# A post-norm transformer layer in fp32 on one core: the products with V in two groups a unit instead of three

## The reference

```python
q, k, v = (einsum('BSE,EHK->BSHK', x, w) for w in (w_q, w_k, w_v))        # 16 heads of 64
logits = einsum('BSHK,BMHK->BSHM', q, k) / sqrt(64)                        # causal mask
o = einsum('BSHM,BMHK->BSHK', softmax(logits + mask, axis=3), v)
x = layernorm(x + einsum('BSHK,EHK->BSE', o, w_o))
h = gelu(butterfly(x @ W_exp + b_exp, up_weights) + up_bias)               # 512 wide, 9 stages
x = layernorm(x + butterfly(h, down_weights) @ W_con + b_con + down_bias)
```

## Time and profile before

| | |
|---|---|
| median of 3 runs | 1035.09 us (1034.93 to 1035.8) |
| the profiled execution | 1035.9 us |
| its span, first to last instruction | 1034.2 us |
| TensorE busy | 1007.0 us, 97% |
| VectorE busy | 778.0 us, 75% |
| GpSimd busy | 750.9 us, 73% |
| ScalarE busy | 613.1 us, 59% |
| mean granted TensorE clock | 0.993 of full |

### The profile page before, as it was taken

One profiled execution on the slowest core, in us unless ns is written; L12 is line 12 of the kernel. 1 busy time (PEld: TensorE's weight loads), 2 busy tenths in 40 slices (PEclk: granted clock), 3 DMA queues, 4 the chain that ended last, 5 costly groups with the idle time before them and its releaser, 6 DMA issues.

```text
span 1034.2 us, 17742 instructions
## 1 busy us (share of the span) xinstructions
PE 1007.0 (97%) x5816; PEld 697.7 (67%) x5816; DVE 778.0 (75%) x2112; ACT 613.1 (59%) x1246; POOL 750.9 (73%) x715
## 2 busy tenths in 40 slices
PE   6799999999999999999999999999999999999997
PEld 4566676676666776676666766767666766765687
DVE  7767777877777777878788778877778888785356
ACT  3555656566656656666556656666555656665544
POOL 6567887777768887777778877777778887777510
PEclk8899999999999999999999999999999999999999
DMA  6233122233222222232232222332222222320002
GB/s 190 62 83 82 45 72 53 62 83 83 58 68 62 63 65 60 63 83 63 70 76 58 62 56 55 83 83 63 66 60 74 63 57 57 83 64 22 22 11 73
DMA packets 48602, 68.71 MB, mean 66 GB/s; under 512 B 15191, under 2 KB 25083, under 8 KB 48510
## 3 DMA queue, kind: packets, MB, share of 16 engines
q1 hardware_dynamic: 48510, 67.57, 25.3%
HBM read 31.11 MB, written 2.36 MB: 32 GB/s over the span
## 4 chain that ended last, share of the span: by engine, by line
PE 92%; DVE 3%; DMA 2%; ACT 1%; issue 1%; POOL 0%; SPq 0%; POOLq 0%; ACTq 0%
PE O L717 25%; PE WORK L631 14%; PE SC L692 14%; PE SC L696 13%; PE WORK L644 6%; PE WORK L679 3%; PE WORK L607 3%; PE WORK L609 3%; PE WORK L608 3%; PE WORK L772 2%; PE WORK L617 1%; PE WORK L619 1%; PE WORK L618 1%; DVE WORK L991 1%; DMA R<-RROW 1%
## 5 line engine op out<-in xcount | busy, mean ns | idle before, releaser
L863 ACT ACTIVATE PR<-SC 128x512 f32<-128x512 f32 (+3 forms) x768 | 352.3, 490 | 263.9 <-PE SC L696 231.4
L519 POOL TENSOR_TENSOR SUM<-SUM,PR 128x1024 f32<-128x1024 f32 (+3 forms) x256 | 419.0, 1637 | 14.8 <-POOL SUM L528 0.5
L991 DVE CUSTOM_DVE_ANT_0 WORK<-WORK,CMASK 128x128 f32<-128x128 f32 (+3 forms) x512 | 239.3, 514 | 65.7 <-PE WORK L631 65.6
L692 PE MATMUL SC<-QH,KHL 128*128 128x512 f32 (+3 forms) x768 | 268.8, 356 | 3.1 <-ACT PR L863 3.0
L696 PE MATMUL SC<-QL,KH 128*128 128x512 f32 (+3 forms) x768 | 261.7, 346 | 3.3 <-DMA QL<-NROW 3.3
L504 POOL TENSOR_SCALAR_AFFINE_SELECT PR<-PR 128x256 f32<-128x256 f32 x256 | 105.9, 415 | 198.0 <-ACT PR L863 197.9
L631 PE MATMUL WORK<-KHL,QH 128*128 128x512 f32 (+3 forms) x768 | 226.5, 365 | 5.9 <-DMA KH<-KHL 4.1
L717 PE MATMUL O<-PR,VLO 128*64 128x512 f32 (+3 forms) x1024 | 200.0, 522 | 0.3 <-DVE OT L1075 0.3
L692 PEld LDWEIGHTS SC<-QH,KHL 128*128 128x128 f32 x768 | 145.2, 189 | 60.7 <-ACT PR L863 28.5
L631 PEld LDWEIGHTS WORK<-KHL,QH 128*128 128x128 f32 x768 | 136.7, 191 | 59.3 <-issue 35.4
L994 DVE TENSOR_REDUCE MP<-WORK 128x1 f32<-128x512 f32 x256 | 164.1, 684 | 4.8
(11 more groups left out here) (132 smaller groups left out, 1099.0 us busy)
## 6 DMA issues: line engine op xcount, KB each, us to landing
QH<-QH SPq DMA_DIRECT2D x128, 128.0 KB, 2.4
KH<-KHL SPq DMA_DIRECT2D x128, 128.0 KB, 2.3
R<-RROW SPq DMA_DIRECT2D x64, 256.0 KB, 3.8
SW<-in_L_ffn_up_weights_dram SPq DMA_DIRECT2D x9, 512.0 KB, 4.4
SW<-_L_ffn_down_weights_dram SPq DMA_DIRECT2D x9, 512.0 KB, 4.3
out_dram<-X SPq DMA_DIRECT2D x7, 256.0 KB, 2.3
X<-in_L_attn_x_BSE_dram SPq DMA_DIRECT2D x3, 512.0 KB, 4.5
X<-in_L_attn_x_BSE_dram SPq DMA_DIRECT2D x2, 256.0 KB, 3.3
```

The lines of the kernel that those rows point to most:

```text
L519: nc.gpsimd.tensor_tensor(total, total, prob(unit, s), ALU.add).then_inc(add_done, 1)
L692: nc.tensor.matmul(dst, KHL[:, par, h, kt * P:(kt + 1) * P], QH[:, par, h, q0:q0 + n], start=True, stop=False)
L863: nc.scalar.activation(prob(unit, s)[:, h, :], SC[use % NSC][:, 0:n], ACT.Exp, scale=K ** -0.5).then_inc(exp_done, 1)
L991: op = nc.vector.tensor_tensor_reduce(cols, cols, CMASK[:, CH - n:], 1.0, LOWEST, ALU.add, ALU.max, cell)
```

## The change

In `PV_AFTER` the products with V of steps 4, 5 and 6 move from behind step 9 to behind step 8, where they join those of steps 0 to 3. There are then two groups a unit: five products behind step 1 and seven behind step 8. In `FILL`, max 15 and 16 move from LATE to BEHIND at step 8, ahead of the products. At step 9, max 18 moves from BEHIND to BETWEEN, so that two maxima lie between the heads and two behind. The ring keeps nine slots.

```diff
-PV_AFTER = {1: [-5, -4, -3, -2, -1], 8: [0, 1, 2, 3], 9: [4, 5, 6]}
+PV_AFTER = {1: [-5, -4, -3, -2, -1], 8: [0, 1, 2, 3, 4, 5, 6]}
 PV_LEFT = [s + NS for ss in PV_AFTER.values() for s in ss if s < 0]
 assert sorted(s % NS for ss in PV_AFTER.values() for s in ss) == list(range(NS))
...
 FILL[7] = [MAXES[11:13], [], MAXES[13:14]]
-FILL[8] = [MAXES[14:15], [], MAXES[15:17]]
-FILL[9] = [MAXES[17:18], MAXES[18:21], []]
+FILL[8] = [MAXES[14:15], MAXES[15:17], []]
+FILL[9] = [MAXES[17:19], MAXES[19:21], []]
 FILL[10] = [[], [("proj", 0, 0)], []]
```

## The result

The changed kernel takes 1093.84 us (median of 4 runs, 1092.79 to 1096.9), against 1035.26 us for the kernel before in the same session (4 runs, 1034.93 to 1035.8). The ratio is 1.0568, with a 95% interval of 1.0554 to 1.0582. It is slower, as predicted, but by 58.6 us instead of 47, which is above the upper end of the range, 1092. The profiled execution took 1092.79 us with a span of 1091.1.

A forecast was written before the change was run, and what follows sets the result against it. TensorE's own work was taken to bound the kernel. The terms -12.8 + 36.3 + 24.2 gave +47.7 us, taken as 47 on 1035.9: 1082.9, against the median 1082 us, with a range of 1057 to 1092.

The forecast's parts named there:

- What bounds the kernel, what a group costs: TensorE's own work bounds the kernel; a group costs 0.40 us beside its columns, so one fewer in 32 units saves 12.8 us.
- The row's wait: TensorE's score waits for the row of maxima, no longer covered by products: 1.11 us in 31 units, +36.3 us with "lay" units.
- The bank's wait: Max 15 and 16, ahead of the products, wait for WORK banks of max 11 and 12: mean 0.82 us, +24.2 us.
- the sizes of the two waits: TensorE's waits per unit: 1.11 us for the row, 0.82 us in the mean for the banks ahead of the products.
- the prediction's rule for the bank's wait: Wait ahead of the group is scale start + 2.12 - (last score matmul + 0.40); summed over 30 units, 24.7 us.
- The bounds: Group gain 9.6 to 14.4 us, row's wait 1.0 to 1.2 a unit, bank's 13.5 to 27 us; likeliest +38 to +54.
- the check from end to end: From step 8's last score to the next unit's first low score: 0.69 us more besides the bank's wait, 46.3 us in all.
- Rival 1: Only the saved switch of a group shows, both waits vanish: faster, 1022.3 us; turns under 0.40 us a unit; 4%.
- Rival 2: Only the row's wait shows, the bank's being met by an earlier scale: 1058.6 us; 10%.
- Rival 3: The clock falls in TensorE's waits, once a unit: +40 us, 1122 us; 3%.
- Rival 4: GpSimd or ScalarE becomes late as well (adds against the norm, step 9's exponentials): up to 0.5 us a unit, 1097; 3%.
- Rival 5: No measurable change, saving and waits in balance; 1%.

The follow-up runs named there:

- Experiment 7: Kernel before with all seven products behind step 9, none behind step 8, and the scale behind step 8's fillers: 1030.32 us, ratio 0.9955.
- Experiment 4: Changed kernel with four extra VectorE transposes into an unread tile, ahead of those that make the row: 1124.53 us, ratio 1.0867.
- experiment 1: Kernel before with only the maxima moved (the edit of `FILL`), products left in three groups: 1062.69 us, ratio 1.0267.
- experiment 3: Changed kernel with the scale one step later, behind the maxima of step 7: 1070.65 us, ratio 1.0345.
- experiment 2: Kernel before with only the products moved (the edit of `PV_AFTER`), fillers left in place: 1073.11 us, ratio 1.0374.
- experiments 7 to 9: Experiment 7, then its kernel with seven products behind step 1 and five behind step 9: 1037.38 us; that with SyncE waiting until the row landed: 1039.44 us.
- experiment 6: Kernel before with four extra VectorE transposes ahead of the row's, and SyncE waiting until the row landed before issuing more DMAs: 1044.46 us, ratio 1.0085.

## Why the prediction was right in direction and short in size

- **What bounds the kernel, what a group costs.** Right. Experiment 7, which adds neither of the two waits, is faster, by 4.65 us of the 12.8; in the unit shown there the entry behind the scale and the products' pace take the rest. 32 groups of seven, and none behind step 9, are seen in the trace.
- **The row's wait, predicted +36.3 us.** The mechanism was right. Its chain came out as predicted (issue to the waiting score 1.84 to 1.87 in 29 of 32 units against 1.86; from the end of the group to the issue 4.61 in units without a "lay", where 0.10 + 0.34 + 0.45 + 3.72 = 4.61 was worked out). In the unit shown TensorE's own way was 5.05 instead of 4.92, mostly because the scores of step 10 took longer, so that it stands for 0.97 and not 1.11; that changes nothing, for the chain sets the stretch. Experiment 4 confirms it from another side: 0.84 more in the chain gave 0.85 more wait.
- **The bank's wait, predicted +24.2 us.** The mechanism and the place were right (experiments 1 and 3). For the unit shown the working gives a group 2.12 + 0.17 + 0.09 after the scale's start, 519.46; it started at 519.57. In a unit with its scale on time the last score to the group takes 1.29, against 0.66 + 0.52 = 1.18.
- **The step that failed: the sizes of the two waits, "TensorE waits 1.11 us" and its twin at the bank.** Over the 30 units of the table the bank's wait, 24.2 in the sum, measures 29.0. The row's, 35.1 for these units, measures 39.6: the other lines of the table give 18.9, to which go the 10.2 of the two maxima that moved and 12.0 for 30 saved groups, less 1.5 for the products' pace. Both priced a wait at its gap alone. The first matmul after a wait takes longer: 530.93 to 531.26 is 0.33 us for 512 columns where 0.23 is the rule. That is 0.10 in each of 31 units, and the stretch to the norm confirms it: 6.83 where the score waited, in the changed kernel and in experiment 2, against 6.72 to 6.73 where it did not, before and in experiment 1. I had the sign of it in hand, since I counted such a 0.10 for the first score behind a group. At the bank it is the same: in all 30 units the group starts 0.37 or 0.38 behind max 16, which has waited (519.20 to 519.57 in the unit shown), where 0.17 + 0.09 = 0.26 was taken. The two make 3.1 + 3.3 = 6.4 us.
- **The smaller terms.** The group of 2816 columns costs 4.88, not 4.83 (1.66 ns a column instead of 1.64): +1.5. The scales were later than in the trace of before: the prediction's rule for the bank's wait, summed over the changed kernel's own scales, gives 26.3 instead of 24.7: +1.6. The clock fell once: +1.4. Three scores started 2.47, 2.11 and 1.95 behind the row's issue: +1.0. With the 6.4 that is 11.9, and 47 + 11.9 = 58.9 against the 58.7 between the first and the last unit. That it meets the 58.6 of the medians so closely is in part luck: the two profiled spans differ by 56.9, and the first low score comes anywhere from 31.4 to 33.7 us in the twelve traces here.
- **The bounds** held each term's gap and none of what follows a wait, so they were too narrow on the upper side: the bank's wait came to 0.97 a unit, above the 0.9, and the row's, with its late landings and the clock, to 1.32, above the 1.2. All the errors listed above have one sign. Two sums of the prediction do not follow from its own terms: its lower bounds add up to +30, not +38, and the check from end to end has 0.78 for a unit with a "lay" where 0.69 + 0.16 is 0.85, which makes it 47.1 instead of 46.3.
- **The rivals.** Rival 1's point of turn (both waits together under 0.40 us a unit) is what experiment 7 reaches. Rival 2 failed, as the bank's wait is there in every unit. Rival 3 happened once in 31, not each time, as this timeline shows with starts 0.43 apart until 98.17:

```profile
95.44 0.80 PE L696 MATMUL SC<-QL,KH 128*128 128x512 f32 x1 [1.34 <-DMA QL<-NROW]
96.03 0.63 PE L692 MATMUL SC<-QH,KHL 128*128 128x512 f32 x1
96.46 0.63 PE L696 MATMUL SC<-QL,KH 128*128 128x512 f32 x1
...
98.17 0.45 PE L692 MATMUL SC<-QH,KHL 128*128 128x384 f32 x1
```

- **Rival 4** did not come: L679 waited for GpSimd once, for 0.9 us. Rival 5 is out.
- **The Trainium skill**, "TensorEngine Tiling (Array Packing)", PSUM Bottleneck, warns of the reading of PSUM after a speed-up by tiling. The trace agrees in so far as TensorE now waits for VectorE's reading of PSUM, 14.8 us in 25 times by the view; but it is the order of the work that brings this about, as experiment 3 shows, and not a faster TensorE.

## What to carry to other kernels

A long block of work that needs nothing from the other engines is also their cover: before merging two blocks, ask which chain ran under each, and place the merged one over the longest chain, late arrivals of it included (experiments 7 to 9). Where covered work has to be done before the block instead, move first what stands ahead of it in the reader's queue (here the scale, worth 23 us). And price a new wait not at its gap alone but with the slower first matmul behind it, the share of cases in which the chain starts late, and the clock; they all add.

## What the runs showed of the hardware that was not expected

- The first 512-column matmul after a wait of TensorE for the row takes 0.33 us to the next start instead of 0.23, at the full clock. A 384-column one that waited for its bank takes 0.11 more as well.
- The clock fell to half (1.2 of 2.4 GHz) after a wait of 1.34 us in one unit of the changed kernel and in seven of 31 units with waits of 1.14 to 2.19 in experiment 4, and not after others as long. Some six matmuls then start 0.43 apart, 1.4 to 1.6 us in all.
- The same 8 KB DMA lands after 1.8 us or, in 7 to 10 of 32 units of four of the kernels, after 3.1 to 3.9. All 32 late ones have a 16 KB packet of an "instruction" queue that begins 1.00 to 1.61 us behind their issue, and land 1.02 to 1.18 us after its end. DMAs issued behind it are not the cause (experiment 6). What holds the DMA up beside such a packet is open.
